# One row of gate passes on TensorE in an attention and recurrence kernel, with a transposition put between two attention products

## What is computed

```python
# attention, for each of the 8 blocks by itself
Q = elu(x @ Wq.T + bq) + 1;  K = elu(x @ Wk.T + bk) + 1;  V = x @ Wv.T + bv
KV = K.T @ V;  Z = Q @ (K.sum(rows) + 1e-6)
x1 = layernorm(x + (Q @ KV / Z) @ Wo.T + bo)
# recurrence over the 8 blocks: one step per block, a state c of 128 for each of the 512 rows
f = sigmoid(x1_t @ wf.T + c @ uf.T + bf);  i = sigmoid(x1_t @ wi.T + c @ ui.T + bi)
g = tanh(x1_t @ wc.T + c @ uc.T + bc);     c = f * c + i * g
h = tanh(x1 @ wo.T + c_final @ uo.T + bo)
out = layernorm(x1 + h)
```

## Time and profile before

| | |
|---|---|
| median of 3 runs | 101.95 us (101.81 to 102.1) |
| the profiled execution | 101.67 us, of which the span from first to last instruction is 99.9 us |
| busy, PE / DVE / ACT / POOL | 90% / 81% / 68% / 43% of the span |
| mean granted TensorE clock | 0.982 of full |
| chain of waits | PE 52%, DVE 31%, issue 4%, ACT 4%, DMA 3% |

### The profile page before, as it was taken

One profiled execution on the slowest core, in us unless ns is written; L12 is line 12 of the kernel. 1 busy time (PEld: TensorE's weight loads), 2 busy tenths in 40 slices (PEclk: granted clock), 3 DMA queues, 4 the chain that ended last, 5 costly groups with the idle time before them and its releaser, 6 DMA issues.

```text
span 99.9 us, 1921 instructions
## 1 busy us (share of the span) xinstructions
PE 90.3 (90%) x607; PEld 77.9 (78%) x607; DVE 80.7 (81%) x236; ACT 67.5 (68%) x141; POOL 42.5 (43%) x61
## 2 busy tenths in 40 slices
PE   5998999999989999999999999999899999977500
PEld 4768779688568978878898899999799999966200
DVE  3155398979999998799589989999837998999970
ACT  1436679479677784967679546759576677898760
POOL 3006288317787228207603812442010134466850
PEclk9999999999999999999999999999999999999975
DMA  2858999100000000000000000000000001233366
GB/s 43 284 211 311 400 393 368 61 0 3 0 0 0 0 0 0 3 7 0 0 0 0 0 0 7 0 3 3 7 0 0 0 0 40 71 105 105 113 202 210
DMA packets 5413, 7.36 MB, mean 74 GB/s; under 512 B 507, under 2 KB 3228, under 8 KB 5404
## 3 DMA queue, kind: packets, MB, share of 16 engines
q1 hardware_dynamic: 4972, 6.92, 19.4%
q10 hardware_dynamic: 432, 0.33, 1.3%
HBM read 5.15 MB, written 2.10 MB: 73 GB/s over the span
## 4 chain that ended last, share of the span: by engine, by line
PE 52%; DVE 31%; issue 4%; ACT 4%; DMA 3%; POOL 1%; DVEq 0%; SPq 0%; ACTq 0%
PE ps_ctx L442 7%; PE ps_ctx L462 5%; PE ps_k L419 5%; PE ps_q L433 5%; DVE stats L1150 4%; DVE s L1020 4%; DMA row<-rows 3%; DVE x L969 3%; DVE x L1166 3%; DVE new L1013 3%; DVE x L984 2%; DVE x_lo L990 2%; DVE x L1139 2%; PE ps_ctx L452 2%; PE ps_x L476 2%
## 5 line engine op out<-in xcount | busy, mean ns | idle before, releaser
L355 POOL TENSOR_TENSOR s_lo<-s,s_hi 128x512 fp32r<-128x512 f32 (+1 forms) x7 | 7.4, 1052 | 21.3 <-ACT s_hi L766 21.3
L342 POOL TENSOR_TENSOR rstd<-var_eps,minus_half 128x4 f32<-128x4 f32 (+1 forms) x9 | 9.0, 1001 | 12.0 <-DVE var_eps L1158 12.0
L326 POOL TENSOR_TENSOR rstd<-var_eps,minus_half 128x4 f32<-128x4 f32 x8 | 8.7, 1091 | 7.9 <-DVE var_eps L960 7.9
L969 DVE TENSOR_SCALAR x<-x,stats,rstd 128x128 f32<-128x128 f32 x28 | 10.3, 423 | 0.0
L317 POOL TENSOR_TENSOR k_pair<-k_rows 128x256 f32<-128x256 f32 x8 | 6.2, 781 | 9.2 <-DVE k_rows L995 9.2
L815 ACT ACTIVATE x_hi<-ps_x 128x512 fp32r<-128x512 f32 x8 | 4.8, 598 | 6.4 <-PE ps_x L476 6.4
L736 ACT ACTIVATE k_exp<-ps_k,minus_one 128x512 f32<-128x512 f32 x8 | 5.5, 686 | 4.9 <-PE ps_k L427 4.0
L419 PE MATMUL ps_k<-wkq,x_cols 128*128 128x128 f32 x64 | 8.6, 278 | 0.0
L433 PE MATMUL ps_q<-x_cols,wkq 128*128 128x512 f32 x16 | 8.2, 593 | 0.0
L419 PEld LDWEIGHTS ps_k<-wkq,x_cols 128*128 128x128 f32 x64 | 7.8, 192 | 0.5 <-DMA wkq<-w_kq 0.4
L984 DVE SCALAR_TENSOR_TENSOR x<-ps_ctx,z_inv,x_rows 128x128 f32<-128x128 f32 x28 | 8.0, 341 | 0.1
(11 more groups left out here) (209 smaller groups left out, 284.1 us busy)
## 6 DMA issues: line engine op xcount, KB each, us to landing
x_cols<-xt SPq DMA_DIRECT2D x8, 256.0 KB, 7.2
x_rows<-x SPq DMA_DIRECT2D x8, 256.0 KB, 7.2
out<-x SPq DMA_DIRECT2D x7, 256.0 KB, 2.2
wgate<-w_gate SPq DMA_DIRECT2D x1, 384.0 KB, 6.6
out<-x SPq DMA_DIRECT2D x2, 128.0 KB, 2.0
wkq<-w_kq ACTq DMA_DIRECT2D x1, 131.0 KB, 3.7
wvo_in<-w_vo_in ACTq DMA_DIRECT2D x1, 128.0 KB, 3.7
wout<-w_out SPq DMA_DIRECT2D x1, 128.0 KB, 6.8
```

The costliest lines, as they stand in the source:

```text
L326: nc.gpsimd.tensor_tensor(rstd[:, b], var_eps[:, b], minus_half[:], ALU.pow).then_inc(rstd_ok, 1)
L342: nc.gpsimd.tensor_tensor(part_of(rstd, u, T), part_of(var_eps, u, T), minus_half[:, 0:nt * H].rearrange("p (t c) -> p t c", c=H), ALU.pow ...
L355: nc.gpsimd.tensor_tensor(s_lo[:, t % 2, part], state(t)[:, part], s_hi[:, t % 2, part].bitcast(F32), ALU.subtract).then_inc(slo_ok[k], 1)
L969: nc.vector.tensor_scalar(x1[:, b, c], x1[:, b, c], mean_of(b, c), rstd[:, b, c:c + 1], ALU.subtract, ALU.mult).then_inc(x1_ok, 1)
```

## The change

In periods 3, 4 and 5 and at the start of the tail, TensorE does `keys_x` directly behind `queries`, then all eighteen gate passes without anything between them, then `key_values`, `x1_turned` (in the loop) and `context`. Before it was `gates_x`, `keys_x`, the forget gate's state passes, `key_values`, the other six passes, `context`, `x1_turned`. In the tail, `keys_x(7)` now follows `key_values(6)`. The instructions are the same ones, and none is added or removed.

VectorE makes `kvo` between `keep` and `new` rather than ahead of `normalise`, and `z_inv` behind `s` rather than ahead of it (periods 3 to 5, and block 6 in the tail). ScalarE makes `s_hi` ahead of the key exponential from period 4 on. GpSimd and SyncE keep their lists.

```diff
@@ TensorE, the loop
                 if t is not None:
+                    keys_x(a)
                     gates_x(t)
-                    keys_x(a)
-                    gate_s(0, t)
+                    gates_s(t)
                 key_values(a)
                 if a == 1:
                     setup_gates()
-                if t is not None:
-                    gate_s(1, t)
-                    gate_s(2, t)
-                context(a)
                 if b >= 2:
                     x1_turned(b)
+                context(a)
 
             keys(7)
             queries(7)
+            keys_x(6)
             gates_x(4)
-            keys_x(6)
-            gate_s(0, 4)
+            gates_s(4)
             key_values(6)
             keys_x(7)
-            gate_s(1, 4)
-            gate_s(2, 4)
             context(6)
             key_values(7)
             x1_turned(5)
@@ ScalarE
+                if t is not None and t >= 2:
+                    state_high(t - 1)
                 key_exp(k)
...
-                if t is not None and t >= 1:
-                    state_high(t - 1)
+                if t == 1:
+                    state_high(0)
...
+            state_high(3)
             key_exp(7)
-            state_high(3)
@@ VectorE
-                if a > 2:
-                    key_values(a)
                 normalise(b)
...
                     kept_state(t)
+                    if a > 2:
+                        key_values(a)
                     new_state(t)
-                    reciprocal_z(a)
+                    if a == 2:
+                        reciprocal_z(a)
                     next_state(t)
+                    if a > 2:
+                        reciprocal_z(a)
...
-            key_values(6)
             normalise(5)
             kept_state(4)
+            key_values(6)
             new_state(4)
+            next_state(4)
             reciprocal_z(6)
             key_values(7)
-            next_state(4)
```

## The result

The changed kernel takes 107.34 us (median of 6 executions, 105.61 to 107.84) against 101.88 before. The six fall in two groups: 105.61 and 105.91, and four from 107.28 to 107.84. The profiled one, 107.28, is of the second group, and the ratio of 1.0384, 95% interval [1.0327, 1.0441], is that of the first alone, 105.8 against 101.9. The trace, which is of the second group, shows TensorE's clock fall; that this is what parts the groups is shown by the experiments. The forecast (106.3, by +4.33) was that of the first group and rival (b), a fall of the clock (107.9), that of the second. I had given it 0.09, and it took four of six.

The account below looks back on a forecast made before the run. TensorE alone was taken to bound periods 4 and 5; after the change VectorE causes its wait. Terms 1.50 + 1.48 + 1.35 = +4.33 on 101.67 gave 106.0, set at 106.3 for the median; 8-in-10 range 104.8 to 107.9.

Parts of the forecast that it names:

- rival (b): Period 3: TensorE idles 2.4 us and its clock falls, costing some 1.6 us more, 107.9; chance 0.09.
- Term 1: Period 3: the keys-rows product waits for two residual instructions, so the last gate comes 1.50 us later.
- Term 2: Periods 4 and 5: the chain through ScalarE and VectorE makes each 9.35 us instead of 8.61, +1.48 together.
- Term 3: Tail: statistics of block 6 come 4.33 us later, 2.98 of it from the loop, so the tail adds +1.35.
- Rival (a): Loop and tail: VectorE is not late, only TensorE's own waits count; +2.5 us, 104.4; chance 0.08.
- (c): Head of period 3: the product fills the wait for `x_lo`, gaining 0.5 us, 101.4 in all; chance 0.02.
- (d): Tail: it runs on VectorE's own work and swallows the loop's delay; no change, 101.95 us; chance 0.02.
- Rival (e): Five waits on the path: weight loads are done under earlier work, 0.1 us less each, 105.8; chance 0.05.

Follow-up runs that it names:

- the kernel with the nine fillers: Nine additional, result-neutral TensorE passes between queries and keys-rows product of period 3, against the changed kernel: 106.07 us.
- the kernels with filled holes: Nine, or four, additional TensorE passes ahead of the keys-rows product of period 3, against the changed kernel: 106.07 and 105.61 us.
- the order without the first edit: Keys-rows product behind the nine x passes again in every period and the tail, against the changed kernel: 104.59 us, ratio 1.0262.
- the first edit alone: Only the keys-rows product moved ahead of the gate passes in periods 3 to 5 and the tail, against the kernel before: 107.35 us.

## Why the prediction was right, and where it was not

The decomposition is best read from the kernel with the nine fillers, where the clock holds; its times are moved by 0.38 (7.98 - 7.60) to the start of the kernel before.

- **Term 1, +1.50.** Its last gate of period 3 came at 34.79, so +1.58.
- **Term 2, +1.48 for two periods.** Measured 9.26 - 8.61 = 0.65 each, +1.30. The chain was right link by link; `x_lo` starts 0.09 behind `z_inv`, not the 0.19 that I took from `z_inv` and `s`.
- **Term 3, +1.35.** From the last gate of period 5 to the statistics 12.79 against 11.45 before: +1.34. One part of it was off: the normalisation took 1.81, not 1.47. It starts directly behind the reciprocal root now and has both key sums of GpSimd beside it. It also began 0.2 nearer to the last gate than I had it, which gave about half of that back; the rest came back in pieces of 0.1 and less behind it.
- **Sum.** +1.58, +1.30 and +1.34 make 4.22, and the distance grew by 58.12 - 53.89 = 4.23; predicted 4.33. The two undisturbed executions of the changed kernel are 3.9 above the median of before, and the kernels with filled holes 4.3 and 3.8.
- **Rival (a)** is out: the bias behind the tanh took 0.8 off, which could not be if only TensorE's own waits counted. **(c)** is out, since the product of period 3 started 2.4 us behind the queries, and **(d)** since the shift of 5.5 at the statistics is the shift of the span.
- **Rival (e)** is out. The two residuals end at 39.85; the product's first load, of rows that had lain ready since the start, began at 39.95 and its first pass at 39.99, though the pass of the queries was in flight until 39.83. The Trainium skill (TensorE: Matmul & The Clock Gate, Architectural detail) states that TensorE can pull a weight load ahead of matmuls in flight. The trace agrees where no wait stands between (the load for L498 began at 40.95, under the pass that began at 40.87), and not for this load behind a semaphore wait.
- **Rival (b), the step that failed.** I priced it at 1.6 (1.46 measured) and set the fall at about 2.4 us of idleness, as it was at the kernel's end; it came at 2.2 and 2.4. But I took the dense work ahead of the hole for protection and gave it 0.09. In two kernels with that hole the clock fell in 9 of 12 executions. The likelier number was therefore 107.9, and 106.3 was the better half of a split. The range held both only because its upper edge had been put at the number of this rival. My own sign of being wrong, "if the granted clock leaves full speed in the loop", came true: of the path and its three terms the forecast was right, of the clock it was wrong.
- **The 2.4 us were luck.** They came from the end of one trace. At the end of the fourteen traces of this study the fall comes 1.7 to 4.8 us after the last pass. The kernel after and the one with nine fillers, whose last passes end at 99.33 and 97.72, have these rows:

```profile
104.00:105.00 1.00, 0.00 (x0) 0.00 (x0) 0.00 (x0) 0.00 (x0) 0.00 (x0) 0.55 0.55 181
```

```profile
99.00:100.00 1.00, 0.00 (x0) 0.00 (x0) 0.70 (x4) 1.00 (x4) 1.00 (x2) 0.72 1.02 336
```

Between full and half speed that is a fall at 104.1, 4.8 after the stop, and at 99.4, 1.7 after it. With such a spread one trace could neither exclude the fall in a hole of 2.4 us nor promise it. What decides it in an execution stays open.
- **A reason that held only by its cover.** "`kvo` is made in the gap ahead of it and costs nothing" is true for the changed kernel. By itself VectorE's order costs 2.6%, and the order without the first edit 2.6% as well, while the first edit alone costs as much as all. The edits share one loss: each makes TensorE late, and a late TensorE hides what the others would cost. Their single prices do not add up.

## What to carry to other kernels

Before an item is moved ahead on a full engine, look up when its last input is ready: what stood ahead of it was the cover of that wait, and everything behind it now waits too. Then follow the loop once round over all engines; its period is the longest such circle, and the busy share of one engine does not tell which that is (TensorE was busy for 88% here, and the circle went over three engines). A long wait on TensorE, 2.4 us here, has a second price, its clock, which is not paid in every execution, so that one trace need not show it; and edits that are judged one by one, or only together, can each give a wrong answer on the others.

## What the runs showed of the hardware that I had not expected

- TensorE's granted clock fell 2.2 to 2.4 us after its last pass though it had been full until then, and was back 3.4 us later (29.0 to 32.4, and 29.5 to 32.9 in the kernel with the one edit). A hole of 1.5 us did not bring the fall in six executions, nor did the wait of 1.45 us of the kernel with VectorE's whole order in its six. At the kernel's end it came 1.7 to 4.8 us after the last pass, in fourteen traces.
- Four normalisations of 128x128 on VectorE take 1.81 us beside the two key sums of GpSimd and 1.11 without them (period 5 of the kernel before, where they start behind the sums). `s`, which reads two SBUF tensors, takes 1.31 beside the weight split and the halving behind it, and 0.69 without them. Two residual instructions, which read one operand from PSUM, take 0.60 with GpSimd's low part of the state at work or without.
- The start of the loop differs by up to 1.3 us between executions (first keys-rows product at 7.60 to 8.86), which is more than the effects of several experiments; it does not enter distances counted from that product.
